# Two weight-piece subtractions moved from VectorE to GpSimd, and one weight load moved behind the row stores

## The reference, cut to what matters

```
x = x + layernorm(softmax(layernorm(x) @ ctx^T / 16, masked) @ ctx) * gamma + beta
h = layernorm(x)
p = softmax(h @ w_gate)                  # 8 experts
p = p * (p in its two largest), divided by its sum
x = x + sum_e p[e] * ((silu(h @ Wg[e]) * (h @ Wu[e])) @ w_down[e])      # Wg, Wu: 256 x 1024, w_down: 1024 x 256
```

## Time and profile before

| | |
|---|---|
| time, median of 3 runs | 433.06 us (432.96 to 433.12) |
| the profiled execution: its own time | 433.62 us |
| the profiled execution: span from first to last instruction | 431.2 us |
| granted TensorE clock, mean of the span | 0.998 |
| PE busy | 420.3 us (97%) |
| DVE busy | 303.7 us (70%) |
| ACT busy | 215.7 us (50%) |
| POOL busy | 196.0 us (45%) |

### The profile page before, as it was taken

How to read it: one execution, slowest core, us unless ns; L and a number is a source line. 1 busy time by engine, 2 the same in 40 slices (tenths; PEclk the granted TensorE clock), 3 DMA queues, 4 the chain that set the end, 5 groups by cost and what they waited for, 6 DMA issues and landing times.

```text
span 431.2 us, 10111 instructions
## 1 busy us (share of the span) xinstructions
PE 420.3 (97%) x2340; PEld 350.1 (81%) x2340; DVE 303.7 (70%) x749; ACT 215.7 (50%) x461; POOL 196.0 (45%) x217
## 2 busy tenths in 40 slices
PE   9999799999999999999999999999999999999995
PEld 6887467888888888888888888888888888888885
DVE  4779988886885678768765568758776568865633
ACT  4886726546554455455633365546544356434431
POOL 6444253564544345644544444445554344444312
PEclk9999999999999999999999999999999999999999
DMA  8778324543454135515531125533552234112212
GB/s 213 215 237 261 126 75 144 152 135 68 131 147 111 26 86 160 132 32 152 151 75 26 25 38 130 165 87 76 146 148 36 39 71 126 27 25 31 33 14 24
DMA packets 28620, 44.16 MB, mean 102 GB/s; under 512 B 2833, under 2 KB 22219, under 8 KB 28587
## 3 DMA queue, kind: packets, MB, share of 16 engines
q1 hardware_dynamic: 20358, 32.96, 25.0%
q0 software_dynamic: 7520, 10.41, 14.3%
q10 hardware_dynamic: 709, 0.32, 0.3%
HBM read 34.04 MB, written 9.65 MB: 101 GB/s over the span
## 4 chain that ended last, share of the span: by engine, by line
PE 88%; DVE 4%; DMA 3%; ACT 2%; SPq 1%; issue 1%; POOL 0%; DVEq 0%; POOLq 0%
PE bank L1462 48%; PE bank L1485 16%; PE bank L1487 8%; PE bank L1475 8%; PE bank L1446 2%; DMA vals<-in_ctx 2%; PE bank L1335 1%; PE bank L1325 1%; DMA tok<-rows_d,gather_i 1%; PE bank L1302 1%; PE bank L1257 1%; PE bank L1532 1%; ACT ctxT L1116 1%; DVE x_sb L706 1%; SPq L428 1%
## 5 line engine op out<-in xcount | busy, mean ns | idle before, releaser
L1462 PE MATMUL bank<-w,tokT_hi 128*128 (+1 forms) x616 | 169.4, 397 | 1.0 <-DVE tokT_lo L927 0.9
L1179 ACT ACTIVATE gated<-bank,row_rstd 128x512 f32<-128x512 f32 x77 | 53.0, 688 | 172.4 <-PE bank L1462 172.4
L1462 PEld LDWEIGHTS bank<-w,tokT_hi 128*128 128x128 f32 x616 | 110.0, 188 | 22.6 <-DVE tokT_lo L927 1.2
L1485 PE MATMUL bank<-w,aT_hi 128*128 (+1 forms) x304 | 116.4, 417 | 0.2 <-DVE w L402 0.2
L936 DVE SCALAR_TENSOR_TENSOR act<-bank,row_rstd,gated 128x512 f32<-128x512 f32 x77 | 57.6, 748 | 77.6 <-ACT gated L1179 77.2
L592 POOL DMA_INDIRECT out<-y_sb,out_i x39 | 62.1, 1592 | 86.3 <-DVE y_sb L957 83.0
L1462 PE MATMUL bank<-w,tokT_lo 128*128 (+1 forms) x308 | 95.4, 391 | 0.0
L1487 PE MATMUL bank<-w,aT_lo 128*128 (+1 forms) x304 | 85.2, 280 | 0.0
L579 POOL TENSOR_TENSOR tok<-tok,beta_b 128x256 f32<-128x256 f32 x36 | 26.2, 728 | 99.5 <-DMA tok<-rows_d,gather_i 99.5
L1462 PEld LDWEIGHTS bank<-w,tokT_lo 128*128 128x128 f32 x308 | 57.8, 188 | 12.6
L1485 PEld LDWEIGHTS bank<-w,aT_hi 128*128 128x128 f32 x304 | 57.2, 188 | 10.5 <-DVE w L402 0.4
(11 more groups left out here) (190 smaller groups left out, 409.9 us busy)
## 6 DMA issues: line engine op xcount, KB each, us to landing
raw<-in_L_ffn_w_gate_up SPq DMA_DIRECT2D x32, 512.0 KB, 3.8
raw<-in_L_ffn_w_down SPq DMA_DIRECT2D x16, 512.0 KB, 3.8
rows_d<-x_sb SPq DMA_DIRECT2D x8, 265.0 KB, 4.7
x_sb<-in_x SPq DMA_DIRECT2D x8, 256.0 KB, 7.5
out<-x_sb SPq DMA_DIRECT2D x8, 256.0 KB, 4.6
out<-y_sb,out_i POOLq DMA_INDIRECT x39, 3.8
tok<-rows_d,gather_i POOLq DMA_INDIRECT x38, 3.8
cap<-in_mask_BxSxS_ik SPq DMA_DIRECT2D x1, 462.0 KB, 6.1
```

What stands on the lines that cost most here:

```text
L1179: act_e.activation(gated[:, h, :], ps_g[h][:, :], ACT.Silu, scale=row_rstd[:, s:s + 1]).then_inc(gated_set, 1)
L1462: ins = pe.matmul(ps[:, :], tokens_[:, s, k, :], w.rearrange("p a g d -> p (a g) d"), start=(k == 0 and tokens_ is tokT_hi and part == 0), ...
L1485: pe.matmul(ps_y[:, :], aT_hi[:, h, c, :], w.rearrange("p a t d -> p (a t d)"), start=(h == 0 and c == 0), stop=False, skip_group_check=True)
```

## The change

Three edits. `split_low(dve, 2)` is taken out of DVE's attention loop and `split_low(dve, 3)` out of its first block. Both are put on POOL, one behind the other, behind the loop that holds the last `scales`, so ahead of the warm-up gather. The load of the sixth piece (`PIECES - 1` is 5) is taken out from between the stores of batches 3 and 4 and put behind the stores of batch 7.

```diff
@@ SP
                 sp.dma_start(out_t[:, b], x_sb[:, tiles(b), 0:D]).then_inc(x1_out, 16)
-                if 1 <= b < 1 + PIECES - RAW:
+                if 1 <= b < PIECES - RAW:
                     load_piece(0, RAW + b - 1)
+            load_piece(0, PIECES - 1)
             with sp.Fori(1, E) as e:
@@ GpSimd
                 scales(i - 1)
                 if i + 1 < B:
                     values_gamma(i + 1)
+            split_low(pool, 2)
+            split_low(pool, 3)
@@ VectorE, attention loop
                 if i == 5:
                     slots(0, GROUPS[0])
-                    split_low(dve, 2)
@@ VectorE, first block
             tok_low(0, 0)
             row_gate(0, 0, 0)
-            split_low(dve, 3)
             own_1, own_2 = expert_of(1), expert_of(2)
```

## The result

The changed kernel takes 437.33 us, the median of 4 runs (435.75 to 437.94), against 433.09 for the kernel before beside it: ratio 1.0093, 95% interval 1.0073 to 1.0114. It is slower by 0.9%, which is 4.2 us by the medians and 4.0 by the ratio; forecast were +3.2 us and 436.3, with a range of 433.7 to 439.3. The profiled execution took 436.92 us, its span 435.2. Some executions of every kernel here were disturbed in the attention stage and took longer; the ratios leave such times out, and as the profiles of e1, e2, e5, e6 and e8 are of disturbed executions, profiles are compared from the last scales on.

The account below looks back on a forecast made before the run. PE was taken to bound the expert stage, with DVE's work between 44 and 47.5 us on the path ahead of it. DVE's waits of +3.35 us less 0.14 for PE gave +3.2, so 436.3 us, range 433.7 to 439.3.

Parts of the forecast that it names:

- What bounds the kernel: PE bounds the expert stage, busy 97% of the span; whatever shifts that stage's start shifts the end by as much.
- Piece 2 gone from DVE: Attention loop: batch 5's scales need 0.69 instead of 1.53 us; at most 0.1 us survives, then worth nothing.
- Piece 3 gone from DVE: First expert block: PE's first projection no longer waits for this instruction; gain 0.14 us, bounds 0 and 0.32.
- The load of piece 5: Load behind batch 7's stores: lands near 52.3 us, cost 0; 0 to 0.3 us if ACT did not shift.
- The subtractions on POOL: Two on POOL behind the last scales, 2.3 us each, 2.05 to 2.46 by a straight line through smaller ones.
- What they do to DVE: Behind the last scales, POOL's subtractions block DVE's two-input SBUF instructions at slots(1) and choose(2); +3.35 us.
- The hand-over between the two subtractions: DVE's L751 gets in between POOL's two subtractions, then x1(7) runs its 0.81 us beside the second.
- Case (a): Rival: POOL streams beside DVE without exclusion, so the gains stand alone; 432.8 us, chance 0.13.
- case (b): Rival: DVE always goes first, POOL finishes late and the first gather starts 1.4 us late; 434.3 us, chance 0.11.
- (d): Rival: piece 5 lands after 55.7 us and ACT stands ahead of the table; chance 0.03, shared with any other.
- the step from 15 ns to 2.2 us: DVE's 15 ns wait for POOL's one-column access becomes about 2.2 us with a 1024-column subtraction.
- rival (c): Exclusion, and PE's clock falls while DVE stands still, slowing spins; +4.8 to +6.4 us, say 438.6 us, chance 0.13.

Follow-up runs that it names:

- e1: Kernel before with piece 2's low part alone on POOL behind the last scales and piece 5's load behind the stores; piece 3 stays on DVE; ratio 1.0063.
- e2: Kernel before with piece 3's low part alone on POOL behind the last scales; piece 2 and the load order unchanged; ratio 1.0145.
- e5: Kernel before, all low parts on DVE, plus four fills of an unused scratch buffer on POOL behind the last scales; ratio 1.0084.
- e6: Changed kernel with each POOL subtraction cut into four of 256 columns; ratio 1.0060 against the kernel before.
- e8: Kernel before with piece 2's low part on POOL inside the attention loop, behind scales(4); the rest unchanged; ratio 1.0029.
- e3: Kernel before with only the load of piece 5 moved behind all stores of rows; 432.35 and 432.77 us, no ratio.
- second profile: The changed kernel profiled once more without any edit; profiled execution 435.46 us, no ratio.
- e4: Changed kernel with more dummy matmuls on TensorE, 14 ahead of the wait for the last x1 and 12 behind; ratio 1.0089 against the kernel before.
- e10: Kernel before without the two times 3 dummy matmuls on TensorE around its wait for the last x1; ratio 1.0012.
- e9: As e1, with 14 dummy matmuls on TensorE ahead of its wait for the last x1 and 6 behind; ratio 1.0048 against the kernel before.

## Why the prediction was right

**What bounds the kernel** held: the 3.5 us lost ahead of the first expert matmul are at the end in full, and e3 and e8, which leave the stretch alone, leave the end alone.

**Piece 2 gone from DVE.** As said: batch 5's scales fall from 1.53 to 0.69 us, and nothing of it survives: `slots(1)` begins at 43.34, 0.16 us ahead of the last scales at 43.50; before it was 43.01, 0.08 us ahead of them.

**Piece 3 gone from DVE.** -0.14 forecast; by the last block TensorE had regained 0.13 us of its distance from the first projection, all of it by block 2's first matmul: 11.89 us behind the first projection, 11.86 in the second profile, 11.94 in e4, 12.03 before. But e2, which takes the same subtraction from DVE, has 12.05 there, and kernels that leave it alone have 11.97 to 12.06. So the number agrees, and that it comes from this removal is not shown. One thing beside it was not foreseen. The 1.2 us of DVE time are not free afterwards, as DVE's timeline of the changed kernel shows:

```profile
63.39 0.17 DVE L984 TENSOR_SCALAR expert_i<-expert_t 1x39 int32<-1x39 int32 x1 [1.31 <-issue]
63.81 0.17 DVE L985 TENSOR_SCALAR weights_t<-expert_f 1x39 int32<-1x39 f32 x1 [0.25 <-issue]
```

Before, the idle time ahead of the first of these was 0.55 us. The loads of `own_1` and `own_2` into registers of DVE's sequencer (`expert_of`, L961 before and L963 here) began at 58.0 us then, under L402, and their last check at 59.8; here they run from 61.9 to 63.3 with nothing beside them, and 1.31 and 0.25 us stand open. Of 1.13 us removed some 0.1 is gained.

**The load of piece 5** cost nothing (e3), and in the changed kernel ScalarE begins its high part at 56.01 us without idle time ahead.

**The subtractions on POOL** take 2.34 us each, against the 2.3 taken from the straight line and its 2.05 to 2.46.

**What they do to DVE** is the step on which all hung, and it was right in kind and in size. The waits are 2.0 us net at L753 and 1.23 at L717, together 3.25, against 3.35 forecast; the clean measure is e4's +3.16. The instruction was one ahead of the one I named: L753, a `tensor_scalar`, was already stopped, not only those with two inputs. The hand-over between the two subtractions happened as assumed, with `x1(7)` beside the second. Case (a), no exclusion, and case (b), one-way exclusion, are excluded by these rows, (d) by e3 and by ScalarE's row.

The way to this step was weaker than its result. The prediction said that POOL's L585 went free "when it started about 0.25 us ahead of L402". In the blocked case at 303.71 us it started 0.25 us ahead as well, and so did four others of the eight; the starts in the record do not tell who had the access first. And the step from 15 ns to 2.2 us on DVE's side was an extrapolation; it is the profiles after the change that show it.

The Trainium skill, "SBUF — State Buffer", section "Who interferes with whom", says that a GpSimd instruction that only writes does not contend with a VectorE instruction that has two SBUF inputs, while VectorE's 2-port modes, which its `tensor_scalar` can enter, contend with GpSimd. The trace of e5 agrees, 0.42 us against 1.19; that L756 ran in such a mode no row shows.

**The clock** is the term that the sum put at nothing. I had it as rival (c), with +1.6 to +3.2 on top, against a forecast of a full clock. It did fall, in the changed kernel's profiles and, by their mean granted clock of 0.989 to 0.990, in all four of its timed runs. But its price in (c) was mis-sized: it is 0.34 us (changed against e4) and 0.55 in the second profile; e10 gives 0.53 by itself. Nothing waits for most of the dummy matmuls that I had counted at half speed, and only the token matmuls ahead of the first gather's index are on the path, 0.32 us of wait there. So the outcome is the forecast's mechanism with a small part of (c): 3.16 + 0.34 - 0.13 = +3.4 us by profiles, +4.2 (+3.2 to +4.9 by the interval) by times. The difference lies within what the attention stage scatters; no run told it apart. So of the 1.0 us between forecast and result the terms explain little: DVE's was 0.1 to 0.2 us too large, the clock's 0.3 to 0.6 was missing, and 0.7 to 0.9 us belong to no term.

## What to carry to other kernels

Before work is moved from VectorE to GpSimd, look at what VectorE does in that time: if it runs two-input or SBUF-to-SBUF scalar operations on the critical chain, the move can cost up to GpSimd's whole duration, though GpSimd is idle (here 3.16 us of 4.67); beside an operation with PSUM and one SBUF input it cost nothing (`x1(7)`), and where VectorE had slack nothing that the stretch behind shows (e8). The trace before often shows it from the other side, in a small GpSimd operation that is sometimes 1.1 us longer. And where one engine's new wait makes TensorE stand still, for 2.6 to 2.9 us here, look at its granted clock behind.

## What the runs showed of the hardware

- A `tensor_scalar` of 12 or 24 columns waits up to 2.2 us for a GpSimd `tensor_tensor` of 128 x 1024 (e1, e2, the change), and about 1 us for a fill of 128 x 1344 that takes 1.22 us (e5).
- A `tensor_tensor` of 128 x 256 with both inputs in SBUF takes 1.65 us beside that subtraction and 0.42 beside the fill.
- The waiting side gets in between two instructions of the other, in both directions: L753 between POOL's two subtractions, and five waits of at most 0.55 us beside eight quarters that take 7.33 us (e6).
- One stillness of TensorE of 2.62 us (e1), 2.68 (e2) or 2.86 (e10) ahead of a short burst was followed by 3 to 6 us at half clock; with dummy matmuls in its place (e4, e9) the clock stayed full.
- Register loads of VectorE's sequencer (L963, 61.9 to 63.3 us) were hidden under a long instruction and came to light, as 1.3 us of idle time, when it was removed.
